# State product of a chunked state-space scan: three fp32r passes over halves in place of one fp32 product

## What is computed

```python
xn = _layernorm(x)
proj = einsum('bld,pd->blp', xn, in_proj_w)          # gate | x, B, C | dt
xBC = silu(causal conv of 4 taps over x, B, C)
dt_p = softplus(dt + dt_bias);  dA = exp(dt_p * A);  dtx = dt_p * x
def step(state, inp):
    state = state * dA_t + dtx_t * B_t                # 128 states x 64 channels per head
    y_t = einsum('bhpn,bhn->bhp', state, C_t)
y = y + x * D;  yn = y * rsqrt(mean(y * y) + eps) * norm_weight * silu(gate)
s = einsum('bli,di->bld', yn, out_proj_w)
out = x + s * silu(ffn(xn))                           # ffn: linear layer with bias and LoRA
```

## Time and profile before

| what | value |
|---|---|
| median of 3 runs | 1795.29 us (1794.1 to 1795.51) |
| profiled execution, its span | 1793.2 us |
| PE busy, PE weight loads busy | 1759.6 us (98%), 1417.5 us (79%) |
| DVE, ACT, POOL busy | 1522.7 us (85%), 836.0 us (47%), 1145.6 us (64%) |
| mean granted clock of PE | 0.998 |
| PE's output product of chunk 3 starts, in two neighbouring groups | 583.60 and 688.64 us |

### The profile page before, as it was taken

How to read it: one execution, slowest core, us unless ns; L and a number is a source line. 1 busy time by engine, 2 the same in 40 slices (tenths; PEclk the granted TensorE clock), 3 DMA queues, 4 the chain that set the end, 5 groups by cost and what they waited for, 6 DMA issues and landing times.

```text
span 1793.2 us, 30683 instructions
## 1 busy us (share of the span) xinstructions
PE 1759.6 (98%) x11416; PEld 1417.5 (79%) x11416; DVE 1522.7 (85%) x1936; ACT 836.0 (47%) x1923; POOL 1145.6 (64%) x1143
## 2 busy tenths in 40 slices
PE   8999999999999999999999999999999999999997
PEld 5778878888887888888777788888888888888875
DVE  7868888888888888888888988889898888989887
ACT  4554453544435354443534434354444535444465
POOL 6537566565756656575697847648574664757567
PEclk9999999999999999999999999999999999999999
DMA  8533333232332323333574333323233332324234
GB/s 267 159 124 113 123 98 133 100 108 105 106 130 87 137 107 106 106 107 124 172 233 143 120 110 127 109 95 123 90 119 117 114 122 94 119 94 129 95 112 147
DMA packets 113508, 220.78 MB, mean 123 GB/s; under 512 B 10448, under 2 KB 46672, under 8 KB 113360
## 3 DMA queue, kind: packets, MB, share of 16 engines
q1 hardware_dynamic: 112320, 218.66, 36.2%
q10 hardware_dynamic: 1040, 0.16, 0.0%
HBM read 204.63 MB, written 14.16 MB: 122 GB/s over the span
## 4 chain that ended last, share of the span: by engine, by line
PE 83%; DVE 8%; ACT 4%; issue 2%; POOL 2%; DMA 1%; SPq 0%; ACTq 0%; DVEq 0%; POOLq 0%
PE ps_conv L1304 9%; PE ps_conv L1307 9%; PE ps_y L1478 6%; PE ps_conv L1310 6%; PE ps_out L1304 6%; PE ps_out L1307 6%; PE ps_gate L1304 6%; PE ps_gate L1307 6%; PE ps_y L1483 5%; PE ps_s L1515 5%; PE ps_out L1310 4%; PE ps_gate L1310 4%; PE turned_x L1395 3%; DVE xc L885 2%; PE ps_conv L1311 2%
## 5 line engine op out<-in xcount | busy, mean ns | idle before, releaser
L885 DVE SCALAR_TENSOR_TENSOR xc<-ps_conv,convw_sb,xc 128x511 f32<-128x511 f32 (+2 forms) x576 | 430.3, 747 | 153.9 <-ACT xc L651 140.3
L1237 POOL TENSOR_TENSOR rstd_col<-mean_square,half 128x1 f32<-128x1 f32 x128 | 89.4, 698 | 533.2 <-ACT mean_square L794 533.2
L1009 DVE TENSOR_TENSOR_SCAN decay<-decay,eye 128x1024 f32<-128x1024 f32 x125 | 294.7, 2358 | 0.9 <-DMA decay<-decays_d 0.9
L657 ACT ACTIVATE xc<-xc 128x512 f32<-128x512 f32 x192 | 121.0, 632 | 322.0 <-DVE xc L885 320.6
L1226 POOL TENSOR_TENSOR cpre<-cpre,xc 128x1024 f32<-128x1024 f32 x112 | 268.8, 2400 | 0.0
L1304 PE MATMUL ps_conv<-xn_hi,wconv_hi 128*128 128x512 f32 x768 | 242.0, 437 | 0.0
L1307 PE MATMUL ps_conv<-xn_hi,wconv_lo 128*128 128x512 f32 x768 | 207.4, 392 | 0.0
L1478 PE MATMUL ps_y<-decay,dtx 128*64 128x128 f32 x1984 | 190.9, 279 | 3.6 <-DVE decay L1030 2.8
L1304 PEld LDWEIGHTS ps_conv<-xn_hi,wconv_hi 128*128 128x128 f32 x768 | 141.4, 194 | 49.3 <-issue 27.2
L803 ACT ACTIVATE square<-ps_y 128x512 f32<-128x512 f32 x126 | 75.6, 600 | 220.8 <-DVE ps_y L1062 220.8
L1483 PE MATMUL ps_y<-cpre,state 128*64 128x128 f32 x1760 | 171.3, 273 | 0.0
(11 more groups left out here) (241 smaller groups left out, 3860.4 us busy)
## 6 DMA issues: line engine op xcount, KB each, us to landing
decay<-decays_d SPq DMA_DIRECT2D x125, 512.0 KB, 5.4
cpre<-rows_d SPq DMA_DIRECT2D x112, 512.0 KB, 3.9
stage<-w_in_t SPq DMA_DIRECT2D x32, 1024.0 KB, 6.6
stage<-w_out_t SPq DMA_DIRECT2D x16, 1024.0 KB, 5.5
stage<-w_in_t SPq DMA_DIRECT2D x32, 256.0 KB, 3.1
out_sum<-hidden SPq DMA_DIRECT2D x16, 256.0 KB, 5.6
ffn_d<-sgate SPq DMA_DIRECT2D x16, 256.0 KB, 2.8
out<-out_sum SPq DMA_DIRECT2D x16, 256.0 KB, 3.6
```

The source lines that it names most:

```text
L885: e.scalar_tensor_tensor(acc[:, d:], ps[:, 0:BLK - d], convw_sb[:, tile, TAPS - 1 - d:TAPS - d], acc[:, d:], ALU.mult, ALU.add).then_inc(S ...
L1009: e.tensor_tensor_scan(d, d, eye8[:, :, :].rearrange("p h i -> p (h i)"), 0.0, ALU.mult, ALU.add).then_inc(scanned(i)[0], 1)
```

## The change

The state product of 105 chunks (groups 0 to 14, steps 0 to 6; `split_state`) is made as hi x hi + lo x hi + hi x lo. ACT copies B a second time (`b_hi`) and copies `xw` to `xw_hi`; POOL subtracts for `b_lo` and `xw_lo`, behind its `rstd_col` and ahead of everything else in the step. The last group (i >= 120) keeps the fp32 product. The DMA scratch argument sizes a ring that no instruction of the kernel uses.

```diff
@@ -77,6 +77,11 @@
     return range(i + CPB - 1, min(i + CPB, N)) if i > 0 else ()
 
 
+def split_state(i):
+
+    return i < SCALED_XW and i % NCH < NCH - 1
+
+
 def linear_at(s):
 
     return s - 4 if 0 <= s - 4 < TOK else None
@@ -189,7 +194,11 @@
         dtx = [sb(f"dtx{i}", [P, GC]) for i in range(2)]
         skip = sb("skip", [P, GC])
         xw = sb("xw", [P, GC])
+        xw_hi = sb("xw_hi", [P, GC], F32R)
+        xw_lo = sb("xw_lo", [P, GC], F32R)
         b_tok = sb("b_tok", [P, NS])
+        b_hi = sb("b_hi", [P, NS], F32R)
+        b_lo = sb("b_lo", [P, NS], F32R)
         square = sb("square", [P, GC])
         square_sum = sb("square_sum", [P, P])
         sgate = sb("sgate", [P, CPB, CPB, P])
@@ -239,7 +248,7 @@
             mm_conv tap0 tail edge_in edge_sum taps silu
             landed_decay0 landed_decay1 landed_decay2 landed_ahead0 landed_ahead1 landed_ahead2 scan_ahead last_ahead
             landed_rows0 landed_rows1 st_rows10 st_rows11 st_rows00 st_rows01
-            mm_t dtx scan last xw mm_bt b_tok mm_g M skip cpre mm_gate sgate mm_in mm_u
+            mm_t dtx scan last xw xw_hi xw_lo mm_bt b_tok b_lo mm_g M skip cpre mm_gate sgate mm_in mm_u
             y state sdec square sum1 sum2 mm_ssq var2 rstd2 yg hi2 lo2 mm_out osum
             landed_io landed_io_apart st_xn0 st_xn1 st_xn2 st_xn3 landed_xn0 landed_xn1 fin1 fin2 last_out stored
             """.split()}
@@ -784,6 +793,8 @@
                 if i < N and at < NCH - 1:
                     w.wait_ge(S["mm_bt"], inner(i))
                     w.wait_ge(S["mm_u"], inner(i) - 1)
+                    if split_state(i):
+                        e.activation(b_hi[:, :], ps_g[:, 0:P], ACT.Copy)
                     e.activation(b_tok[:, :], ps_g[:, 0:P], ACT.Copy).then_inc(S["b_tok"], 1)
                 if u >= 0:
                     w.wait_ge(S["mm_ssq"], u + 1)
@@ -793,6 +804,10 @@
                         w.wait_ge(S["mm_bt"], inner(i))
                     e.activation(mean_square[:, u % 2:u % 2 + 1], ps_g[:, 2 * P:2 * P + 1], ACT.Identity, bias=eps[:, :],
                                  scale=1.0 / GC).then_inc(S["var2"], 1)
+                if split_state(i):
+                    w.wait_ge(S["xw"], inner(i))
+                    w.wait_ge(S["mm_u"], inner(i) - 1)
+                    e.activation(xw_hi[:, :], xw[:, :], ACT.Copy).then_inc(S["xw_hi"], 1)
                 if 0 <= m < N:
                     w.wait_ge(S["y"], m + 1)
                     w.wait_ge(S["sum2"], m)
@@ -1235,6 +1250,11 @@
                     w.wait_ge(S["var2"], u + 1)
                     w.wait_ge(S["osum"], u - 1)
                     e.tensor_tensor(rstd_col[:, col], mean_square[:, col], half[:, :], ALU.pow).then_inc(S["rstd2"], 1)
+                if split_state(i):
+                    w.wait_ge(S["b_tok"], inner(i))
+                    e.tensor_tensor(b_lo[:, :], b_tok[:, :], b_hi[:, :].bitcast(F32), ALU.subtract).then_inc(S["b_lo"], 1)
+                    w.wait_ge(S["xw_hi"], inner(i))
+                    e.tensor_tensor(xw_lo[:, :], xw[:, :], xw_hi[:, :].bitcast(F32), ALU.subtract).then_inc(S["xw_lo"], 1)
                 if i < N:
                     g, at = divmod(i, NCH)
                     left = BATCH * GROUPS - 1 - g
@@ -1509,10 +1529,19 @@
                     conv(conv_late(i))
                 if i < N and i % NCH < NCH - 1:
                     w.wait_ge(S["pt"], 3 if i < 3 else 4)
-                    w.wait_ge(S["b_tok"], inner(i))
-                    w.wait_ge(S["xw"], inner(i))
                     w.wait_ge(S["state"], inner(m) if m >= 0 else 0)
-                    e.matmul(ps_s[:, :], b_tok[:, :], xw[:, :], start=True, stop=True).then_inc(S["mm_u"], 1)
+                    if split_state(i):
+                        w.wait_ge(S["b_tok"], inner(i))
+                        w.wait_ge(S["xw_hi"], inner(i))
+                        e.matmul(ps_s[:, :], b_hi[:, :], xw_hi[:, :], start=True, stop=False)
+                        w.wait_ge(S["b_lo"], inner(i))
+                        e.matmul(ps_s[:, :], b_lo[:, :], xw_hi[:, :], start=False, stop=False)
+                        w.wait_ge(S["xw_lo"], inner(i))
+                        e.matmul(ps_s[:, :], b_hi[:, :], xw_lo[:, :], start=False, stop=True).then_inc(S["mm_u"], 1)
+                    else:
+                        w.wait_ge(S["b_tok"], inner(i))
+                        w.wait_ge(S["xw"], inner(i))
+                        e.matmul(ps_s[:, :], b_tok[:, :], xw[:, :], start=True, stop=True).then_inc(S["mm_u"], 1)
                 if i < N and conv_late(i) is not None and not late_first:
                     conv(conv_late(i))
                 if i + 1 < N:
@@ -1549,7 +1578,7 @@
         "ffn_bias": lay(L0_ffn_bias),
         "lora_w": lay(np.repeat(np.asarray(L0_ffn_lora_weights), LORA_R)).reshape(LORA_N * LORA_R, 1),
     }
-    nc = bacc.Bacc("TRN2", target_bir_lowering=False, num_devices=1)
+    nc = bacc.Bacc("TRN2", target_bir_lowering=False, num_devices=1, dynamic_dma_scratch_size=1024)
     args = [nc.dram_tensor(name, a.shape, mybir.dt.from_np(a.dtype), kind="ExternalInput").ap()
             for name, a in arrays.items()]
     out = nc.dram_tensor("out", (BATCH, SEQ, DM), F32, kind="ExternalOutput").ap()
```

## The result

The changed kernel takes 1862.48 us (median of 4 runs, 1860.34 to 1864.37), the kernel before, run beside it, 1795.4 (4 runs, 1794.1 to 1796.87). The ratio is 1.037, with a 95% interval of 1.0361 to 1.0387: slower by 67 us, where 1860 was forecast. The profiled execution took 1863.61 us with a span of 1861.8, so 68.6 more than the span before.

What follows compares the result with a forecast made beforehand. PE was taken to set the time, with waits added. 13 ordinary groups +54, group 0 +3.5, group 7 +6, group 8 +2.5: +66 on the 1793.2 span, plus 2.1, gives 1861, rounded to 1860 us; range 1810 to 1882.

Steps and rivals of the forecast that it cites:

- step 3: Fourth chunk step of a group: POOL's cpre ends late, so PE's output product starts 3.5 us late on the old clock.
- group 8: POOL still finishing the first batch's outputs: 2.5 us beyond its 4.15, counted apart.
- Step 1: Second chunk step: late xw and the subtractions put cpre's end at 662.6, making PE 0.7 us late.
- the coupling: Lateness carried through steps 0 to 2 by edges, skip and y: step 3's DVE chain 1.5 us late, PE only 0.5.
- The second wait: After step 3's output product, PE waits for POOL's second sum of squares, held up by DVE's scan: 1.2 us.
- 12 ordinary groups: Groups away from start, end and batch turn: +4.15 us each; the prediction counted 13, group 8's 4.15 included, for +54.
- group 0: First group, which already lost 0.6 us to DVE at this place: +3.5 us.
- group 7: POOL also finishes the first batch's outputs and cpre already holds PE up for 0.80 us: +6 us.
- Local waits: Rival: idle time in DVE and ACT keeps waits from carrying across steps; 1813 to 1840 us, chance 0.25 for 1808 to 1840.
- Faster: Rival: subtractions fit into POOL's 533 us of idle time and PE keeps its 19 us saving; 1776 us, chance 0.09.
- `cpre` behind the scan: Rival: in step 3 DVE's scan goes first and cpre stands 2.3 us; about 1875 us, chance 0.13 including more boundary loss.
- Slower passes: Rival: PE's new passes run slower than other fp32r ones, a few tenths each, hidden or +10 us; no chance of its own.

Runs made afterwards that it cites:

- a1: Changed kernel without POOL's two subtractions, all three passes using the high halves: 1779.47 us, 0.9919 of the kernel before.
- c1: Changed kernel splitting only the products of steps 4 to 6, those of group 7 left in fp32: 1785.67 us, 0.9945 of the kernel before.
- c3: Changed kernel with edge sums moved to step 7, products of steps 1, 3 and the batch turn left fp32: 1783.15 us, 0.9933 of the kernel before.
- c4: As c3 but with step 1 split too, 83 products: 1801.07 us, 1.0027 of the kernel before.
- a3: Changed kernel with the product split everywhere but in step 3 of each group: 1812.42 us, 1.0103 of the kernel before.
- b2: Changed kernel with POOL's edge sums moved from step 0 to the end of step 7: 1854.65 us, 1.0336 of the kernel before.
- a4: Changed kernel with the product split in step 3 of each group alone, 15 products: 1847.5 us, 1.0298 of the kernel before.
- b1: Changed kernel with POOL's four conv splits moved from step 3 to the end of step 2: 1825.65 us, 1.0174 of the kernel before.
- b3: Changed kernel with POOL's two sums of squares ahead of cpre in step 3: 1913.31 us, 1.0663 of the kernel before.
- b4: Changed kernel with edge sums in step 7, two conv splits in step 2, one output split ahead of step 1's reciprocal root: 1806.36 us, 1.007 of the kernel before.

## Why the prediction was right, and where its parts were off

The mechanism came as forecast: `cpre` of step 3 ends too late for PE, the scan then meets it and delays the second sum, and steps 0 to 2 make step 3 late. What failed is the working for group 8, and the clock, which it left out; both are below.

**The gain on PE.** 0.17 to 0.20 per product was forecast; it is 0.17 before the transposes and 0.23 before a conv tile (a1, c1). I had read the product's price up to the start of the second group of pieces behind it; up to there the saving is 0.21 (1.79 against 1.58 in c1), and another 0.02 comes in the two groups of pieces after that. An estimate from the four passes that the Trainium skill counts for true fp32 (FP8 and Floating Point Precision, TensorE Precision Notes) gives 0.22 or 0.23, which the trace bears out before a conv tile, not before the transposes.

**POOL.** 105 x (1.294 + 0.460) = 184 us of subtractions, as forecast (186), but POOL is busy 232 us more, not 186. The other 48 are mostly instructions that stand behind a scan, since a standing instruction counts as busy: the 128 `skip` have 178.9 us for 133.3, the first sums of squares 128.1 for 98.7, while the state decays stand less (114.1 for 130.1). The scans of over 3.7 us are 15, as forecast, from 3.77 to 3.79.

**Step 1 and the coupling.** The forecast on the old clock holds link by link. With the lateness of the groups ahead (21.58 us) taken off, chunk 1's output product of group 5 starts at 662.67 (forecast 662.65; -0.17 and +0.89 in the table make the same 0.72), `skip` ends at 667.74 (667.8), `y` starts 1.86 late (1.9) and the next scan 1.54 late (1.5). It is the right place by c3 and c4, and a3's +0.75 in step 3 is this coupling alone. Its two roads can be told apart: with the edge sums moved (b2) the same scan is 0.82 late instead of 1.54, but PE is 0.7 earlier too. It is step 1's own subtractions ahead of the output splits that put `skip` behind the scan, and they alone make the increment at step 3.

**Step 3.** `cpre` was to end 4.1 us later on the old clock; in group 4 it ends at 602.96 against 582.92, which is 20.04 later in a group ahead of which PE had lost 16.01: 4.03. The output product's +3.01 (forecast 3.5 - 0.5) and the scan's 3.79 (3.82 forecast) are right to 0.05. The second wait was put at 1.2; at full clock it costs 1.17 in a4 and 1.15 in the change (0.98 with the product's 0.17 counted off). Its cause, the scan, is shown by b1 (no overlap, no wait) and b3. The Trainium skill (SBUF, State Buffer; Who interferes with whom) says that a vector instruction with two SBUF inputs and a GpSimd instruction that reads SBUF block each other; the trace agrees: the scan began 1.64 us before `cpre` ended and ended 1.51 late.

**The sum** is nearer than its parts, and that is luck: their errors, -1.3, +5.4, +0.4, +1.3 and -3.0, partly cancel.

| term | forecast | measured |
|---|---|---|
| 12 ordinary groups, full clock | 49.8 (4.15 each) | 48.5 (4.04) |
| the slower clock in 7 of them | 0 | 5.4 |
| group 0 | 3.5 | 3.9 |
| group 7 | 6 | 7.3 |
| group 8 | 6.65 | 3.6 |
| sum | 66 | 68.7 |

The step that failed is group 8's "2.5 beyond its 4.15": it costs less than an ordinary group, since its step 3 came only 0.89 later behind steps 1 and 2 that had already lost 1.75 and 0.55. In the kernel before this group took 108.3 us instead of 105.0, and PE stood in it for 1.02 us ahead of chunk 2, waiting for DVE's mixing matrix; in the change that wait is gone, so part of the new lateness fell into it. Whether that is the whole reason is open. Group 0's 3.9 has another make-up than its forecast too: its step 1 loses 2.83, where an ordinary group loses 0.89, and a1, without the subtractions, gains 0.25 there. That is the `b_lo` that waits for B ahead of ready work, which I had not seen. (The first output product of the run starts from 1.6 us earlier to 1.4 later in these kernels, which is in group 0's sums.) And the clock was missing, 5.4 us put at nothing: I had not asked what 3 us of idle time do to PE's speed.

**The rivals.** Local waits (1813 to 1840): a3 still loses 0.75 at a step 3 that is not split, so the coupling is real; a4, with step 3 alone, loses 3.19 per group, and the two together are nearly the change's 4.03. Faster (1776): this is what a1 gives (1779), so the rival was right on PE and wrong on POOL's two instructions. `cpre` behind the scan (1875): b3 is near this case, and at 1913 it is dearer than I had priced, since there `square_sum` stands and `cpre` behind it, and the clock falls. Slower passes: none, since the three take 0.69 us in the change.

## What to carry to other kernels

An engine with a third of its time free can still be the wrong place for helper work: what counts is the slack in the step where the work goes and what stands queued behind it. Here the same change costs 67 us when every product is split, and gains 12 (0.7%, clear of the interval) when the two steps in which GpSimd is full and the turn between the batches are left out and the edge sums stand a step earlier. Before moving work onto a helper, list for each step how early it delivers what others wait for, and see which long vector instruction its instructions will meet (here the scan); and compare kernels by the lateness that each step adds, since a total hides terms that cancel.

## What the hardware did that I had not expected

- After PE had stood for 3.1 us in the middle of full load, the next matmuls ran at the 1.2 GHz level in some groups and not in others (windows of 0.77 and 1.00 around the same place); after 6.3 us it was so in each of the twelve ordinary groups of b3 (0.77 to 0.80 in the window). In a4 the same followed 2.1 us of standing still, in eight of twelve groups. Waits of the same length so cost 0 to 1.5 us more.
- The mutual exclusion of DVE and POOL reaches the smallest instructions: DVE's `last` of 0.17 us took 0.51 behind a sum of squares and 1.07 behind a weight split (b4), and POOL's `square_sum` of 0.46 took 2.44 behind a scan (b3). An instruction that meets a scan pays for the rest of the scan, whatever its own size.
